# Two expert layers: the second product with features on partitions, gates spread by a 0/1 product, sums on GpSimd

## The reference, cut to what matters

```
probs = softmax(x @ gate_w + gate_b); idx = argmax(probs); prb = probs[idx]
pos = (cumsum(one_hot) * one_hot).sum(-1) - 1;  kept = pos < C
hmid = relu(buf @ w1[e] + b1[e]);  ybuf = hmid @ w2[e] + b2[e]
y = ybuf[idx, pos] * (prb * kept)          # then nan_to_num, added to h, layer norm
```

```
topk_w = softmax(top_k(x @ gate_w + gate_b, 2))
h = relu(x @ w1[e] + b1[e]);  expert_out = h @ w2[e] + b2[e]
y = x + sum(topk_w * expert_out[topk_idx])   # then layer norm with gamma, beta
```

## Time and profile before

| what | value |
|---|---|
| median of three runs | 3146.17 us |
| the profiled execution | 3139.24 us |
| its span in the trace | 3137.6 us |
| TensorE matmul, busy | 2607.6 us (83%), 32240 instructions |
| VectorE, busy | 2033.2 us (65%) |
| ScalarE, busy | 1634.0 us (52%) |
| GpSimd, busy | 670.4 us (21%) |
| mean granted TensorE clock | 0.939 |

### The profile page before, as it was taken

The page is one execution under the profiler, slowest core; times in us unless marked ns, Lnnn a source line. Parts: engine busy times, 40 slices in busy tenths (PEclk is TensorE's granted clock), DMA queues, the critical chain, the costliest instruction groups (busy, mean ns, idle before and its releaser), DMA issues.

```text
span 3137.6 us, 82394 instructions
## 1 busy us (share of the span) xinstructions
PE 2607.6 (83%) x32240; PEld 1691.8 (54%) x32240; DVE 2033.2 (65%) x3091; ACT 1634.0 (52%) x1951; POOL 670.4 (21%) x402
## 2 busy tenths in 40 slices
PE   4677688899778899789899788999999969954994
PEld 2333356566556666566566543444444349952893
DVE  4888667788657788658888544555555452256557
ACT  4556444455335555335555346777777824422451
POOL 2332322323213232223322212311111110000000
PEclk9988999999989999999999898999999988986897
DMA  2523345745346755446655412241111000000000
GB/s 65 155 90 115 87 176 177 227 177 185 123 154 197 216 181 185 141 140 205 219 181 185 129 57 81 64 101 52 61 51 56 29 1 1 1 1 1 1 1 14
DMA packets 130762, 335.92 MB, mean 107 GB/s; under 512 B 66694, under 2 KB 94630, under 8 KB 94758
## 3 DMA queue, kind: packets, MB, share of 16 engines
q1 hardware_dynamic: 108070, 161.53, 16.7%
q10 hardware_dynamic: 18432, 134.23, 10.7%
q0 software_dynamic: 4096, 37.75, 5.5%
HBM read 179.30 MB, written 154.14 MB: 106 GB/s over the span
## 4 chain that ended last, share of the span: by engine, by line
PE 70%; DVE 13%; issue 6%; ACT 6%; DMA 4%; POOL 1%; SPq 1%; DVEq 0%; ACTq 0%; POOLq 0%
PE pA L1364 15%; PE pA L1374 8%; PE pT L1445 7%; PE pS L1416 6%; PE pT L1387 5%; PE pD L1434 4%; PE pD L462 4%; PE pA L462 3%; PE pD L1401 3%; ACT w_sb L1499 3%; DVE arena L1724 2%; PE pS L454 2%; PE pT L454 2%; PE pT L1459 2%; DVE h_rows L1714 2%
## 5 line engine op out<-in xcount | busy, mean ns | idle before, releaser
L1158 POOL TENSOR_TENSOR w_sb<-w_sb,small 128x1024 f32<-128x1024 f32 x320 | 608.4, 1915 | 1688.2 <-DVE small L208 1687.5
L1364 PEld LDWEIGHTS pA<-conv_bd,h_in 128*128 128x128 f32 x4096 | 496.8, 198 | 143.1 <-ACT w_sb L1499 65.1
L1364 PE MATMUL pA<-conv_bd,h_in 128*128 128x128 f32 x4096 | 535.8, 286 | 38.6 <-DMA h_in<-h_scratch 23.8
L1520 ACT ACTIVATE h_new<-pT,bet,gam 128x1024 f32<-128x1024 f32 x256 | 308.2, 1204 | 336.0 <-PE pT L1387 300.8
L1683 DVE TENSOR_REDUCE small<-arena 128x32 f32<-128x1056 f32 x320 | 390.0, 1219 | 138.4 <-ACT arena L1509 136.4
L1499 ACT COPY w_sb<-pA 128x1024 f32<-128x1024 f32 x256 | 258.9, 1011 | 328.1 <-PE pA L1374 280.1
L1387 PE MATMUL pT<-cst,w_sb 128*128 128x128 f32 x2048 | 291.0, 287 | 92.0 <-ACT h_new L1520 48.2
L1714 DVE STREAM_TRANSPOSE h_rows<-h_new 128x1024 f32<-128x1024 f32 x256 | 310.6, 1229 | 74.0 <-ACT h_new L1520 72.8
L1387 PEld LDWEIGHTS pT<-cst,w_sb 128*128 128x128 f32 x2048 | 229.3, 146 | 219.6 <-POOL w_sb L1158 95.1
L1509 ACT ACTIVATE arena<-w_sb 128x1024 f32<-128x1024 f32 x320 | 337.7, 1055 | 6.8 <-DVE w_sb L1676 2.7
L1374 PE MATMUL pA<-arena,cst 64*64 64x256 f32 x4096 | 282.7, 392 | 0.0
(11 more groups left out here) (299 smaller groups left out, 3594.0 us busy)
## 6 DMA issues: line engine op xcount, KB each, us to landing
h_scratch<-h_new ACTq DMA_DIRECT2D x128, 1024.0 KB, 4.2
h_in<-h_scratch SPq DMA_DIRECT2D x128, 1024.0 KB, 5.0
y_scratch<-w_sb POOLq DMA_DIRECT2D x32, 576.0 KB, 8.2
y_in<-y_scratch SPq DMA_DIRECT2D x512, 36.0 KB
w_sb<-in_L_tok_w1r_dram POOLq DMA_DIRECT2D x8, 576.0 KB, 6.7
w_sb<-in_L_tok_w1i_dram POOLq DMA_DIRECT2D x8, 576.0 KB, 6.9
w_sb<-in_L_tok_w2r_dram POOLq DMA_DIRECT2D x8, 576.0 KB, 6.5
w_sb<-in_L_tok_w2i_dram POOLq DMA_DIRECT2D x8, 576.0 KB, 6.6
```

Source lines behind the costliest of these rows:

```text
L1158: pool.tensor_tensor(z, z, r.broadcast_to([P, 32, C]), ALU.mult).then_inc(s["normed"], 1)
L1364: pe.matmul(pA[:, c:c + 128], h_in[:, 1024 * n + c:1024 * n + c + 128], conv_bd[:], start=(j == 0), stop=False, skip_group_check=True)
L1520: act.activation(h_new[:, 1024 * n:1024 * n + 1024], pT[:], ACT.Gelu if ph == "mid" else ACT.Identity, bias=bet[:, col], scale=gam[:, col] ...
```

## The change

The second product is turned round. For expert e and a step u of 1024 tokens, `output` now takes 64 columns of w2 as weights and 512 tokens of `hid` as the moving part, so that features lie on partitions: the first 512 tokens of the step (r = 0) write partitions 0 to 63 of a bank, the next 512 (r = 1) partitions 64 to 127. First products run `ahead` steps in front (2 in layer 1, 4 in layer 2).

The gates must then be a row along tokens, the same on 64 partitions. TensorE turns them (`gates_turned`, four chunks of 1024 tokens), ScalarE writes them rounded to G_split (`upper`), VectorE writes the rest below (`lower`), and for each (e, u) one f32r product with a 0/1 matrix of expert e (`picks`) spreads them over 64 partitions for each half (`gates_spread`). VectorE copies the spread out of PSUM and multiplies the second product by it into one of four buffers ZT; GpSimd adds ZT to YT. The products with b2 now come first and are copied into YT. At the end TensorE turns YT back and VectorE adds it to X. The six passes for NaN run on YT. GpSimd builds `picks` once from a constant of 32 columns.

```diff
-                def output(e, k, b):
+                def output(e, u):
+                    b = bank("d")
+                    for h in range(H):
+                        for r in range(2):
+                            slot = ((e * 4 + u) * 2 * H + r * H + h) % 8
+                            mm = pe.matmul(b[64 * r:64 * r + 64, :], w2[:, (e * H + h) * S:(e * H + h) * S + S], hid[slot],
+                                           start=(h == 0), stop=(h == H - 1))
+                    sent("d", mm)
+
+                def gates_turned(u):
+                    b = bank("d")
                     for i in range(4):
-                        for h in range(H):
-                            slot = ((e * 8 + k) * H + h) % 8
-                            mm = pe.matmul(b[:, S * (4 * (k % 2) + i):S * (4 * (k % 2) + i) + S],
-                                           hid[slot][:, 128 * i:128 * i + 128], w2[:, (e * H + h) * S:(e * H + h) * S + S],
-                                           start=(h == 0), stop=(h == H - 1))
-                    return mm
+                        for c in range(4):
+                            at_gate = E * (8 * u + 4 * (c % 2) + i)
+                            mm = pe.matmul(b[32 * c:32 * c + 32, 128 * i:128 * i + 128], gates[:, at_gate:at_gate + 32], ident,
+                                           start=True, stop=True)
+                    sent("d", mm)
+
+                def gates_spread(e, u):
+                    if e == 0:
+                        pe.wait_ge(s["g_lower"], (0 if E == E1 else 4) + u + 1)
+                        bias(u)
+                    b = bank("d")
+                    sent("d", pe.matmul(b[:], picks[:, P * e:P * e + P].bitcast(F32R), G_split[:, 512 * u:512 * u + 512].bitcast(F32R),
+                                        start=True, stop=True))
+
+                def bias(u):
+                    b = bank("d")
+                    sent("d", pe.matmul(b[:], b2, G_split[:, 512 * u:512 * u + 512], start=True, stop=True))
 
                 pe.wait_ge(s["w1_split"], 2 if E == E1 else 4)
-                todo = [(e, k) for e in range(E) for k in range(8)]
-                ahead = 8 // H - 1
-                for block in todo[:ahead]:
-                    hidden(*block)
+                pe.wait_ge(s["picked"], 1)
+                todo = [(e, u) for e in range(E) for u in range(4)]
+                ahead = 4 // H
+                for e, u in todo[:ahead]:
+                    hidden(e, 2 * u)
+                    hidden(e, 2 * u + 1)
...
-                for i, (e, k) in enumerate(todo):
+                pe.wait_ge(s["gated"], 1 if E == E1 else 2)
+                gates_turned(0)
+                gates_turned(1)
+                gates_spread(0, 0)
+                for i, (e, u) in enumerate(todo):
+                    if i < 2:
+                        gates_turned(i + 2)
+                    if i + 1 < len(todo):
+                        gates_spread(*todo[i + 1])
+                    taken("s", 2 * H * min(ahead - 1, len(todo) - 1 - i))
+                    output(e, u)
                     if i + ahead < len(todo):
-                        hidden(*todo[i + ahead])
...
+                        for r in range(2):
+                            hidden(todo[i + ahead][0], 2 * todo[i + ahead][1] + r)
...
+                pe.wait_ge(s["combined"], 1 if E == E1 else 2)
+                for u in range(4):
                     b = bank("d")
-                    sent("d", pe.matmul(b[:], GT[0:8 * E, 128 * j:128 * j + 128], b2[0:8 * E, :], start=True, stop=True))
+                    for i in range(4):
+                        mm = pe.transpose(b[:, 128 * i:128 * i + 128], YT[:, 512 * u + 128 * i:512 * u + 128 * i + 128], ident)
+                    sent("d", mm)
```

On ScalarE (`upper` stands behind the relus of the first products that run ahead, and chunks 2 and 3 behind four and eight relus more in layer 1, two and four in layer 2):

```diff
+                def upper(u):
+                    d = D_GATES[0 if E == E1 else 1] + (u if u < 2 else 4 * u - 4)
+                    act.wait_ge(s["td_full"], d + 1)
+                    act.copy(G_split[:, 512 * u:512 * u + 512].bitcast(F32R), TD[d % 4][:]).then_inc(s["g_upper"], 1)
                 for i in range(E * 8 * H):
+                    if i == 8:
+                        upper(0)
+                        upper(1)
+                    if i in (8 + 2 * H, 8 + 4 * H):
+                        upper(2 if i == 8 + 2 * H else 3)
```

On VectorE, `combine` and the end:

```diff
+                lower(0)
+                lower(1)
+                copied = gate_copied(0)
+                for i in range(4 * E):
+                    if i < 2:
+                        lower(i + 2)
+                    ready = copied
+                    if i + 1 < 4 * E:
+                        copied = gate_copied(i + 1)
+                    out = take()
+                    dve.wait_ge(s["td_free"], ready)
+                    if before + i >= 4:
+                        dve.wait_ge(s["z_free"], before + i - 3)
+                    dve.tensor_tensor(ZT[i % 4], out[:], gate_rows[i % 4], ALU.mult).then_inc(s["td_free"], 1)
+                dve.wait_ge(s["z_free"], before + 4 * E)
...
+            def add_turned(out, x):
+                v = lambda a, u: a.rearrange("p (u h i x) -> p u i h x", u=4, h=2, x=S)[:, u]
+                for u in range(4):
+                    b = take()
+                    dve.tensor_tensor(v(out, u), v(x, u), b[:].rearrange("p (i h x) -> p i h x", h=2, x=S), ALU.add).then_inc(s["td_free"], 1)
...
-            link(dve.tensor_tensor(X, X, Y, ALU.add))
+            dve.sem_inc(s["combined"], 1)
+            add_turned(X, X)
```

On GpSimd:

```diff
+                if n == 0:
+                    pool.tensor_copy(picks[:].bitcast(F32R).rearrange("p (e m) -> p e m", m=S),
+                                     const["pick"].rearrange("p (e o) -> p e o", o=1).broadcast_to([P, 2 * E2, S])).then_inc(s["picked"], 1)
+            for layer, E in enumerate((E1, E2)):
+                before = 0 if layer == 0 else 4 * E1
+                for i in range(4 * E):
+                    c = slice(512 * (i % 4), 512 * (i % 4) + 512)
+                    pool.wait_ge(s["td_free"], gated_products(layer, i, E))
+                    if before + i >= 4:
+                        pool.wait_ge(s["z_free"], before + i - 3)
+                    pool.tensor_tensor(YT[:, c], YT[:, c], ZT[i % 4], ALU.add).then_inc(s["z_free"], 1)
```

More of the change, by code:

```diff
@@ L43 @@
 CAPACITY = 1.25
-N_PARAMS = 23 + 16 + 12
+N_PARAMS = 23 + 8 + 12
 HUGE = 3.0e38
@@ L113, in constants @@
     put("falling", np.tile(np.arange(E2, 0, -1), (P, 1)))
+    pick = np.zeros((P, E2, 2))
+    for p in range(P):
+        if p % C < E2:
+            pick[p, p % C, p // C % 2] = 1
+    put("pick", pick.reshape(P, 2 * E2))
     return np.concatenate(parts, 1).astype(np.float32)
@@ L326, in build @@
         late = param(P, NC_COLS - NC_EARLY)
+        assert at_col[0] <= M1 * KX * B
         const |= {k: late[0:r, a - NC_EARLY:a - NC_EARLY + n] for k, (a, r, n) in CONST_COLS.items() if a >= NC_EARLY}
@@ L335, in build @@
         w1b_lo = rounded("w1b_lo", "spec", E1 * F1 + E1 * F1 // P * S, E2 * F2)[:]
+        picks = rounded("picks", "h_new", 0, E2 * P)
+        G_split = rounded("G_split", "arena", 0, 2048)
         QT, KT = arena[0:64, 0:4096], arena[0:64, 4096:8192]
@@ L345, in build @@
         tiny = [w_sb[:, 4096 + 512 * i:4608 + 512 * i] for i in range(8)]
-        gates = arena[:, 8192:8704]
-        GT = arena[:, 8704:9216]
+        gates = arena[:, 8192:8736]
+        YT = h_in[:, 0:2048]
+        ZT = [h_in[:, a:a + 512] for a in (2048, 2560, 3072, 3584)]
+        gate_rows = [Z2[:, a:a + 512] for a in (0, 512, 1024, 1536)]
         GA, GZ = arena[:, 0:2048], arena[:, 2048:4096]
@@ L360, in build @@
                   "exped", "e_subbed", "fc1_bias", "mlp_ready", "w1_split", "upper", "e_exped", "gated", "acc_done", "out_stored", "wg_scaled",
-                  "scored", "gru_act", "gru_out", "ones_set", "passed"]
+                  "scored", "gru_act", "gru_out", "ones_set", "passed", "g_upper", "g_lower", "picked", "combined", "z_free"]
         s = {n: sem(n) for n in names}
@@ L588, in build, with gated_products @@
         d_attn = 8 + 8 + 4 + 4
-        d_ffn = 1 + 2 + E1 * 4 + NT // 8
+        d_ffn = 1 + 2 + 4 + 4 + 2 * 4 * E1 + 4
         GRU_D = [d_attn + d_ffn, d_attn + d_ffn + 4]
+        D_GATES = [d_attn + 1 + 2, GRU_D[1] + 4 + 4 + 1]
+        def gated_products(layer, i, E):
+            taken = 2 + min(i + 1, 2) + min(i + 2, 4) + min(i + 2, 4 * E) + i + 1
+            return D_GATES[layer] + taken + 4
         s_attn = 8 + 8 + 8
-        s_ffn = 8 + E1 * 8 * (F1 // P) + 1
+        s_ffn = 8 + E1 * 8 * (F1 // P)
         S_TURNED = [s_attn, s_attn + s_ffn + 1 + 8 + 8]
@@ L676, in combine @@
             def combine(E):
[L678 to L688, removed]
@@ L689, in combine, with lower @@
-                link(dve.memset(tiny[2][:, 0:1], 0.0))
-                for j in range(4):
-                    b = take()
-                    c = slice(512 * j, 512 * j + 512)
```

(38 more changed lines are left out.)

16 lines of the change are left out of this document (1 added, 15 removed).

## The result

The changed kernel takes 3112.43 us, the median of eight runs (3103.39 to 3118.76). In the same comparison the kernel before has a median of 3144.12. The ratio is 0.9916, 95% interval 0.9897 to 0.9936: some 26 us, less than 2%. The forecast was 3064 with a range of 3030 to 3104, so the time lies outside the range, and about a third of the forecast gain is there. (The ratio is not the quotient of the two medians: three of the eight runs of before, at 3288 to 3293 us, were disturbed and are left out of it.)

A forecast was written before the change was run, and what follows sets the result against it. TensorE's work was taken to bound both expert loops. Gains of 42.1 and 33.3 us in the layers plus 1.2 and 1.9 at the ends make 78.5, from 3139.24 to 3060.7; with the median 6.9 higher, forecast 3064, range 3030 to 3104.

The forecast's parts named there:

- two halves run side by side, 0.43 a pair: Second product: matmuls on the two column halves overlap, 0.43 us a pair; 0.86 if they did not.
- Layer 1 pays 1.01 a step, layer 2 one pair: Second product's cost in a step of 1024 tokens: 1.01 us in layer 1, 0.58 in layer 2.
- the steps that the forecast counted as steady: Loop steps after the start, with 29 and 61 second products counted: 3.25 us in layer 1, 1.91 in layer 2.
- the clock's return: Expert loops after their starts: 2 us in each layer until TensorE is back at full clock.
- rival 3: Second product: the halves do not overlap, 55 us more, 3119 us; chance 0.06.
- Shapes: Tile shape changes twice a step: 0.19 us, besides 0.15 inside the second product's 1.01.
- What must hide under the step: ScalarE's relus, VectorE's copy and product (1.46 us), GpSimd's sum (at most 1.3) all fit under TensorE's step.
- Rival 2: VectorE or GpSimd sets layer 2's pace at 2.27 us a step, 23 us more, 3087 us; chance 0.15.
- The starts: Each layer's beginning, waiting for gates at half clock: first output at 2621.2 and 2923.8, then two long rounds.
- rival 1: The layers' starts run at full clock, 17 us more gain, 3047 us; chance 0.20.
- The ends: End of each layer, old gate work removed and final transposes added: gains of 1.2 and 1.9 us.
- Rivals 4 and 5: 4: clock stays low in the loops, 3244 us, chance 0.05; 5: loops keep their time through unseen wait, 3146, 0.04.

The follow-up runs named there:

- e2: Changed kernel with both token halves of the second product written to the same 64 output partitions: 3219.85 us in one run.
- e1: Changed kernel with the second product of both layers in float32r, 128 weight columns, output not the reference's: 3025.74 us, ratio 0.963 to the kernel before.
- e3: Changed kernel with all four gate chunks turned, rounded and subtracted before a layer's first output: 3095.5 us, ratio 0.9865 to the kernel before.
- e4: Changed kernel with the sums over the experts back from GpSimd on VectorE: 3108.19 us, ratio 0.9903 to the kernel before.
- e5: Changed kernel with all gate chunks first and layer 2's second product in float32r with zero-padded weights: 3042.63 us, ratio 0.9719 to the kernel before.
- e6: Changed kernel with all gate chunks first and both layers' second products in float32r with zero-padded weights: 3006.05 us, ratio 0.9588 to the kernel before.

## Why the prediction was wrong, point by point

**The step that failed is the second product: "two halves run side by side, 0.43 a pair", "Layer 1 pays 1.01 a step, layer 2 one pair".** The four records of L1445 in the earlier trace rows were read as four matmuls, two pairs. They are two matmuls of the code, one pair, two instructions each. So a pair costs 0.86, and the step's cost was taken at half its size. That is 2 x 0.43 = 0.86 too little in layer 1 and 0.43 in layer 2, and nearly all of the excess of the steps (0.90 and 0.47). Over the steps that the forecast counted as steady this makes 29 x 0.90 + 61 x 0.47 = 54.8 us. The shortfall is 78.5 - 25.9 = 52.6: these 54.8, the 3.4 between the layers, and 5.6 that came out better, most of it the 2 us a layer put in for the clock's return, which no row gave: in the trace after, the first products stand 0.23 apart, as at the full clock, right behind the third output in both layers. The evidence was there before: a block of layer 1 has 4*H = 8 second products in the code, and the earlier trace rows show x16. The 0.47 read from four records of L495 in the earlier trace rows is half a matmul in the same way. The blocks of before were measured whole, so this did no harm there; it did where a record was carried over to code that had not run.

The Trainium skill, "FP8 and Floating Point Precision", TensorE Precision Notes, says that true FP32 takes four passes through the array. The trace agrees in time, though it shows two records and not four: two of 0.43 make 0.86 us, 3.8 times the 0.227 of one float32r matmul over the same 512 columns. By an estimate from the page, four passes of 0.227 would have put the pair at 0.91.

**That halves overlap** was right (e2), and rival 3 is out, although the changed kernel's time lies near its 3119: the right-looking number came from another cause. The rule of the Trainium skill weighed in the prediction ("TensorE: Matmul & The Clock Gate", Part 3), that a weight load overlaps matmuls only with another row group, is still not borne out: eight loads of 0.13 us and eight matmuls share 1.87 us, of which the matmuls, two abreast and 0.43 apart, fill 1.72 and the change of shape the rest.

**Shapes.** Forecast: 0.19 and the 0.15 inside the 1.01, so 0.34 a step. Measured: 4.15 - 9 x 0.228 - 2 x 0.86 = 0.38 and 2.38 - 5 x 0.228 - 0.86 = 0.38. Right to 0.04; e1, with one shape, has none of it.

**What must hide under the step** did. GpSimd's sum takes 1.29 (forecast at most 1.3); the group of its sums, and what it waited for (us, times):

```profile
L910 POOL TENSOR_TENSOR h_in<-h_in x96: 1259/1286/1302, 2620.6 to 3054.4; 128x512 f32<-128x512 f32 x96
...
DVE h_in L759: 349.5, 95
```

It waits for VectorE's product before nearly every sum (1.08 us of a step of 2.38 in layer 2, above; the 349.5 also hold the time between the layers). Rival 2 is out.

**The starts** came out close, partly by luck. The end of the gates in layer 1, after:

```profile
2604.41 0.42 DVE L812 TENSOR_TENSOR arena<-arena,w_sb 128x256 f32<-128x256 f32 x1
```

From the gates to the first output it is 7.15 us in layer 1 (2604.83 to 2611.98), where the forecast had 6.15 (2615.05 to 2621.2), with rounds of 10.2 and 8.9 (9.7 and 9.05). In layer 2 it is 6.65 (6.16), with rounds of 6.7 and 5.9 (7.2 and 6.3). But the clock is 0.87 and 0.86 in these stretches, not half: it lies between the forecast and rival 1. And a chunk of gate transposes is 32 records for 16 matmuls, the same miscount: 1.7 us for each of the first two in layer 1, where 0.86 was forecast. The two errors work against each other. What holds the rounds is as described, PE waiting for VectorE's subtraction; e3 shows it by removing it.

**The ends** were right. The timeline after, the last second products and the normalization's first sum in both layers:

```profile
2749.31 1.89 PE L473 MATMUL pA<-w_sb,spec 128*64 128x512 f32 x8
...
2770.42 2.29 DVE L680 TENSOR_REDUCE w_sb<-w_sb 128x32 f32<-128x2048 f32 x1
...
3051.31 1.94 PE L473 MATMUL pA<-w_sb,spec 128*64 128x512 f32 x8
...
3059.01 2.29 DVE L680 TENSOR_REDUCE w_sb<-h_new 128x32 f32<-128x2048 f32 x1
```

From the end of the one to the start of the other it is 19.2 and 5.8 us. Before it was 20.5 (2779.33 to 2799.81) and 7.9 (3086.96 to 3094.86), so 1.3 and 2.1 less; the forecast was 1.2 and 1.9.

**Not of the change:** 3.4 us between the layers, in code that did not change. Most of them, 2.2, lie in the score products of layer 2; before, after, and in e4, which has the changed kernel's code there:

```profile
2894.74 10.99 PE L447 MATMUL pA<-spec,XT_split 128*128 128x16 f32 x64 [1.42 <-DVE XT_split L674]
```

```profile
2866.55 13.17 PE L457 MATMUL pA<-spec,XT_split 128*128 128x16 f32 x64 [1.42 <-DVE XT_split L724]
```

```profile
2879.73 11.04 PE L457 MATMUL pA<-spec,XT_split 128*128 128x16 f32 x64 [1.42 <-DVE XT_split L724]
```

The same 64 records take 13.17 us where the clock is 0.55 (2866 to 2880), and 10.99 and 11.04 where it is 0.66 (2894 to 2906; 2879 to 2891). The whole stretch of the table is 117.1 us before and 120.5 after, 120.8 in e2, but 116.9 to 117.8 in e1, e3, e4, e5 and e6. So the forecast of 0 was right, and the 3.4 are a matter of the single execution: the clock rose later in two of eight traces. Why in these two stays open.

Rivals 4 and 5 are out: the loops run at 1.00, and both are shorter than before (32 x 4.15 = 133 and 64 x 2.38 = 152 us, against 173.6 each).

## What to carry to other kernels

Before a record of one line is used as the price of another, divide the count of records by the count of matmuls in the code: a float32 matmul here is two instructions. A float32 matmul of 64 output columns pays off by running beside its other half, 0.43 us for each of the two. In float32r, with 128 columns of weights of which half are zero, it takes 0.227, at the price of rounding; float32r on two halves side by side was not tried. When a loop begins behind a late input, prepare all chunks of that input before the first step, if the steps would otherwise wait for them one at a time.

## What the runs showed of the hardware

- A float32 matmul of 512 columns: two instructions, 0.43 us each at the clock of 1.00 (e2); float32r: one of 0.227 (e1). With 64 output columns in each, eight float32 instructions take 1.94 us on two halves of the partitions and 3.65 on one (durations in the traces of after and e2).
- A sum of two 128x512 tiles takes GpSimd 1.29 us, 0.15 more than a quarter of its 4.53 for 2048 columns, and VectorE 0.69.
- The same 64 untouched score products took 11.0 us in some executions and 13.2 in others, at a mean clock of 0.66 and 0.55; a difference of this size between two single traces is not yet an effect of a change.
